# New instruction orders in a one-core conv-attention and recurrence kernel: the softmax and normalisation stages

## The reference

```python
x = x + conv(ln_c(x))                # x: 16 x 32 x 32 x 32, fp32
#   q, k, v = Wq x, Wk x, Wv x       (over channels c)
#   weight = softmax(q k / d + Gq q rq / d + Gk k rk / d)     over the last axis
#   conv   = weight (Gv1 v) + weight (Gv2 rv)
t = tokens(x)                        # 16 x 1024 tokens x 32
t = t + ffn(ln_t(t))                 # Wx = batchnorm(W ln_t(t)); y_t = sigmoid(Wx_t + V y_(t-1))
```

## Time and profile before

| | us |
|---|---|
| median of 3 runs | 154.19 (152.92 to 155.33) |
| time of the profiled execution | 154.99 |
| its span, first to last instruction | 153.1 |
| busy in the span: PE, DVE, ACT, POOL | 101.6, 96.2, 73.6, 61.9 |
| scores start (L990) | 40.13 |
| first addition of the softmax (L742) | 48.11 |
| first `weighted_sums` matmul (L1043) | 74.13 |
| first `residual` (L782) | 86.76 |
| last `bn_part` starts (L820) | 122.11 |

### The profile page before, as it was taken

How to read it: one execution, slowest core, us unless ns; L and a number is a source line. 1 busy time by engine, 2 the same in 40 slices (tenths; PEclk the granted TensorE clock), 3 DMA queues, 4 the chain that set the end, 5 groups by cost and what they waited for, 6 DMA issues and landing times.

```text
span 153.1 us, 4782 instructions
## 1 busy us (share of the span) xinstructions
PE 101.6 (66%) x2063; PEld 70.5 (46%) x2064; DVE 96.2 (63%) x158; ACT 73.6 (48%) x161; POOL 61.9 (40%) x62
## 2 busy tenths in 40 slices
PE   0769978686598880999755950358208987999400
PEld 0313312475588770888655950112002336999400
DVE  5996874000304879705501896379988969888992
ACT  8957786347700236692230030332343449999500
POOL 8995439840000687740500054555343000003940
PEclk9999999999779999599999999557965999999965
DMA  4880899899000002434332000000000000000467
GB/s 138 294 206 0 189 206 237 192 226 188 12 4 4 4 4 54 106 75 101 91 90 58 4 4 0 2 0 0 0 0 0 4 0 0 0 6 0 144 197 208
DMA packets 9825, 11.67 MB, mean 76 GB/s; under 512 B 2828, under 2 KB 6924, under 8 KB 9804
## 3 DMA queue, kind: packets, MB, share of 16 engines
q1 hardware_dynamic: 9612, 10.84, 28.0%
q10 hardware_dynamic: 192, 0.52, 1.4%
HBM read 2.97 MB, written 2.10 MB: 33 GB/s over the span
## 4 chain that ended last, share of the span: by engine, by line
DVE 27%; PE 18%; SPq 15%; ACT 13%; issue 11%; DMA 8%; POOL 5%; POOLq 0%; ACTq 0%
SPq L286 7%; PE ps L1033 5%; PE ps L990 5%; ACT warm L658 4%; DMA gates<-in_L_conv_Gk_dram 4%; SPq L291 4%; DVE xin L351 3%; DMA v_tile<-u_tile 3%; PE ps L1043 3%; DVE stat L786 3%; DVE y_tile L357 3%; DVE u_tile L782 2%; DVE rel_tile L816 2%; PE ps L1020 2%; ACT v_tile L658 2%
## 5 line engine op out<-in xcount | busy, mean ns | idle before, releaser
L1054 PE MATMUL ps<-rel_tile,w_bd 128*128 128x512 f32 x16 | 12.6, 888 | 10.9 <-DVE rel_tile L816 10.9
L357 POOL TENSOR_TENSOR y_tile<-xin,u_tile 128x256 f32<-128x256 f32 (+1 forms) x7 | 7.1, 1049 | 23.6 <-DVE xin L351 23.6
L990 PE MATMUL ps<-spread,v_tile 128*32 128x64 f32 x512 | 13.5, 269 | 4.4 <-DMA v_tile<-u_tile 3.0
L407 POOL TENSOR_TENSOR att_tile<-att_tile,soft 128x1024 f32<-128x1024 f32 x4 | 7.8, 1946 | 19.1 <-DVE soft L746 19.1
L990 PEld LDWEIGHTS ps<-spread,v_tile 128*32 128x32 f32 x512 | 12.6, 195 | 5.4 <-issue 4.5
L757 DVE TENSOR_TENSOR u_tile<-ps,xin 128x512 f32<-128x512 f32 x8 | 5.5, 684 | 15.0 <-PE ps L1033 15.0
L596 ACT ACTIVATE square<-y_tile 128x512 f32<-128x512 f32 x8 | 4.9, 629 | 18.4 <-POOL y_tile L428 18.4
L428 POOL TENSOR_TENSOR y_tile<-u_tile,stat 128x512 f32<-128x512 f32 x7 | 7.3, 1048 | 15.6 <-DVE stat L788 15.6
L1043 PE MATMUL ps<-spread,v_tile 128*32 128x64 f32 x512 | 9.2, 223 | 6.4 <-issue 6.4
L887 DVE TENSOR_SCALAR ps<-att_tile,bnv 128x512 f32<-128x512 f32 (+1 forms) x18 | 12.3, 762 | 1.2 <-ACT warm L658 1.1
L1020 PE MATMUL ps<-w_bd,y_tile 128*32 128x128 f32 x256 | 9.2, 307 | 5.0 <-ACT v_tile L510 5.0
(11 more groups left out here) (103 smaller groups left out, 234.1 us busy)
## 6 DMA issues: line engine op xcount, KB each, us to landing
spread<-rel_tile SPq DMA_DIRECT2D x32, 64.0 KB, 2.0
out_dram<-y_tile SPq DMA_DIRECT2D x8, 256.0 KB, 2.3
xin<-in_x_dram SPq DMA_DIRECT2D x3, 512.0 KB, 4.9
spread<-att_tile SPq DMA_DIRECT2D x12, 128.0 KB, 3.5
v_tile<-u_tile SPq DMA_DIRECT2D x12, 128.0 KB, 3.1
xin<-in_x_dram SPq DMA_DIRECT2D x2, 256.0 KB, 2.8
...
```

The costliest lines, as they stand in the source:

```text
L357: return eng.tensor_tensor(result[:, :, rows, :], back[:, at:at + P * k].rearrange("p (q i j) -> p q i j", q=Q, i=k), x2[:, :, rows, :], A ...
L407: nc.gpsimd.tensor_tensor(att_m[:, n, :, :], att_m[:, n, :, :], soft[:, 0, n, :].unsqueeze(2).broadcast_to([P, C, C]), ALU.subtract).then_ ...
L990: return nc.tensor.matmul(ps[group(g), first + j // 8, at:at + Q * HALF].rearrange("p (q i) -> p q i", q=Q), u_by_q[:, g, :, j], y_bd[:, : ...
L1054: nc.tensor.matmul(bank(WX_BANK[k % 2]), w_bd[:, 1, :], by_row(tokens, k), start=True, stop=True).then_inc(S["wx_product"], 1)
```

## The change

The order of calls is changed on every engine. The load of `rv` is issued after `regroup_u(2)`. The small multiplication that made a mean on DVE is gone: where DVE centres, one `scalar_tensor_tensor` computes sum * (-1/32) + x from the broadcast sum, and where POOL centres, POOL first makes the mean with a `tensor_scalar` on 128x32 or 128x16 and waits for it. `score_max` is split in two, `score_add` and `score_max`. The transfers of the weights are issued by SP, in both kernels and in the same order. The diff, cut to its core:

```diff
@@ block.sync
             spread_y(1)
-            for g in range(G):
-                sp.dma_start(rv_in[group(g), :], rv.rearrange("c h i -> c (h i)")).then_inc(S["rv_in"], 16)
             regroup_u(1)
             spread_y(2)
             spread_y(3)
             regroup_u(2)
+            for g in range(G):
+                sp.dma_start(rv_in[group(g), :], rv.rearrange("c h i -> c (h i)")).then_inc(S["rv_in"], 16)
@@ block.gpsimd
-            pool.wait_ge(S["ln_mean"], 3)
-            ln_centre(nc.gpsimd, 2, "ln_centred")
+            def ln_centre(n):
+                q = LN_PARTS[n][0]
+                pool.wait_ge(S["ln_sum"], n + 1)
+                nc.gpsimd.tensor_scalar(stat[:, 1, q, :], stat[:, 0, q, :], 1.0 / C, None, ALU.mult).then_inc(S["ln_mean"], 1)
+                pool.wait_ge(S["ln_mean"], q)
+                nc.gpsimd.tensor_tensor(centred[:, q, :, :], xin[:, q, :, :], stat[:, 1, q, :].unsqueeze(2).broadcast_to([P, C, C]),
+                                        ALU.subtract).then_inc(S["ln_centred"], 1)
...
             def centre(k):
+                pool.wait_ge(S["t_sum"], k + 1)
+                nc.gpsimd.tensor_scalar(stat2[:, 1, k, :], stat2[:, 0, k, :], 1.0 / C, None, ALU.mult).then_inc(S["t_mean"], 1)
                 pool.wait_ge(S["t_mean"], k + 1)
...
             centre(1)
+            centre(2)
+            centre(3)
             scale(0)
-            centre(2)
             scale(1)
-            centre(3)
             scale(2)
@@ block.scalar
             t_std(3)
+            t_square(4)
+            t_square(5)
+            t_std(4)
             wx_out(0)
+            t_std(5)
             wx_out(1)
...
@@ block.vector
-                dve.wait_ge(S["ln_sum"], n + 1)
-                dve.wait_ge(S["nought_set"], 1)
-                nc.vector.scalar_tensor_tensor(out=stat[:, 1, q, rows], in0=stat[:, 0, q, rows], scalar=1.0 / C,
-                                               in1=nought[:, 0:k], op0=ALU.mult, op1=ALU.add).then_inc(S["ln_mean"], 1)
...
+                nc.vector.scalar_tensor_tensor(out=centred[:, q, rows, :],
+                                               in0=stat[:, 0, q, rows].unsqueeze(2).broadcast_to([P, k, C]), scalar=-1.0 / C,
+                                               in1=xin[:, q, rows, :], op0=ALU.mult, op1=ALU.add).then_inc(S["ln_centred_dve"], 1)
...
+            score_add(0)
             score_max(0)
+            score_add(1)
             score_max(1)
             weight_sum(0)
+            score_add(2)
             weight_sum(1)
             score_max(2)
+            score_add(3)
             score_max(3)
             weight_sum(2)
-            relv_out(0)
-            relv_out(1)
             weight_sum(3)
...
-                dve.wait_ge(S["t_sum"], k + 1)
-                nc.vector.scalar_tensor_tensor(out=stat2[:, 1, k, :], in0=stat2[:, 0, k, :], scalar=1.0 / C,
-                                               in1=nought[:, 0:HALF], op0=ALU.mult, op1=ALU.add).then_inc(S["t_mean"], 1)
                 if k == UNITS - 1:
-                    nc.vector.tensor_tensor(unit(x2n, k), unit(x2, k),
-                                            stat2[:, 1, k, :].unsqueeze(2).broadcast_to([P, HALF, C]),
-                                            ALU.subtract).then_inc(S["t_centred_dve"], 1)
+                    nc.vector.scalar_tensor_tensor(out=unit(x2n, k), in0=stat2[:, 0, k, :].unsqueeze(2).broadcast_to([P, HALF, C]),
+                                                   scalar=-1.0 / C, in1=unit(x2, k), op0=ALU.mult, op1=ALU.add
+                                                   ).then_inc(S["t_centred_dve"], 1)
@@ block.tensor
-            for n in range(4):
+            for n in range(PIECES4):
                 relative_values(n)
             pe.wait_ge(S["score_sum"], CHUNKS)
             pe.wait_ge(S["att_in0"], 16 * Q * G)
             weighted_sums(0, range(C)).then_inc(S["wsum_product"], 1)
-            for n in range(4, PIECES4):
-                relative_values(n)
```

More of the change, by code:

```diff
@@ L170, in side_bank @@
             return bank(SIDE[n % 2])
-        def ln_centre(eng, n, done):
-            q, row, k = LN_PARTS[n]
-            eng.tensor_tensor(centred[:, q, row:row + k, :], xin[:, q, row:row + k, :],
-                              stat[:, 1, q, row:row + k].unsqueeze(2).broadcast_to([P, k, C]),
-                              ALU.subtract).then_inc(S[done], 1)
         def ln_scale(eng, n, done):
@@ L572, in _ @@
             score_exp(1)
-            turn_weights(0)
-            turn_weights(1)
             value_out(0)
             value_out(1)
-            score_exp(2)
+            turn_weights(0)
             value_out(2)
             value_out(3)
+            turn_weights(1)
+            value_out(4)
+            score_exp(2)
+            value_out(5)
+            value_out(6)
             score_exp(3)
-            value_out(4)
-            value_out(5)
+            value_out(7)
             turn_weights(2)
-            value_out(6)
-            value_out(7)
             turn_weights(3)
@@ L682, in ln_mean, with ln_centre @@
                 nc.vector.tensor_reduce(stat[:, 0, q, rows], xin[:, q, rows, :], AX_X, ALU.add).then_inc(S["ln_sum"], 1)
+            def ln_centre(n):
+                q, row, k = LN_PARTS[n]
+                rows = slice(row, row + k)
                 dve.wait_ge(S["ln_sum"], n + 1)
-                dve.wait_ge(S["nought_set"], 1)
-                nc.vector.scalar_tensor_tensor(out=stat[:, 1, q, rows], in0=stat[:, 0, q, rows], scalar=1.0 / C,
-                                               in1=nought[:, 0:k], op0=ALU.mult, op1=ALU.add).then_inc(S["ln_mean"], 1)
+                nc.vector.scalar_tensor_tensor(out=centred[:, q, rows, :],
+                                               in0=stat[:, 0, q, rows].unsqueeze(2).broadcast_to([P, k, C]), scalar=-1.0 / C,
+                                               in1=xin[:, q, rows, :], op0=ALU.mult, op1=ALU.add).then_inc(S["ln_centred_dve"], 1)
             def ln_sum2(n):
@@ L702, in ln_out @@
                 ln_scale(nc.vector, n, "y_ready_dve")
-            ln_mean(0)
-            dve.wait_ge(S["ln_mean"], 1)
-            ln_centre(nc.vector, 0, "ln_centred_dve")
-            ln_mean(1)
-            dve.wait_ge(S["ln_mean"], 2)
-            ln_centre(nc.vector, 1, "ln_centred_dve")
-            ln_mean(2)
+            ln_sum(0)
+            ln_centre(0)
+            ln_sum(1)
+            ln_centre(1)
+            ln_sum(2)
             ln_sum2(0)
@@ L716, in _ @@
             ln_out(1)
-            ln_mean(3)
+            ln_sum(3)
             ln_sum2(2)
@@ L824, in _ @@
             residual(2)
+            residual(3)
             t_sum2(0)
-            residual(3)
+            t_sum2(1)
             t_rstd(0)
-            t_sum2(1)
+            t_sum2(2)
             t_rstd(1)
-            t_sum2(2)
+            t_sum2(3)
+            t_rstd(2)
+            t_rstd(3)
+            residual(4)
+            residual(5)
             t_turn(0)
-            t_rstd(2)
-            t_sum2(3)
-            t_rstd(3)
             t_turn(1)
-            residual(4)
+            t_sum2(4)
             t_turn(2)
-            residual(5)
+            t_rstd(4)
+            t_sum2(5)
             t_turn(3)
+            t_rstd(5)
+            residual(6)
+            residual(7)
             bn_part(0)
-            residual(6)
-            t_sum2(4)
+            t_sum2(6)
             bn_part(1)
-            t_rstd(4)
-            residual(7)
-            t_sum2(5)
-            t_rstd(5)
-            bn_part(2)
-            t_turn(4)
-            t_sum2(6)
             t_rstd(6)
             t_sum2(7)
+            t_turn(4)
+            t_rstd(7)
+            bn_part(2)
             t_turn(5)
             bn_part(3)
-            t_rstd(7)
             t_turn(6)
```

31 lines of the change are left out of this document (11 added, 20 removed).

## The result

The change makes the kernel faster: 145.75 us (median of 4 runs, 145.43 to 146.24) against 154.76 (4 runs, 152.92 to 155.95), a ratio of 0.949 with the interval 0.941 to 0.958. The medians here are of all runs, while each ratio and its interval leave out the runs that lie more than 1.5% above the fastest of their kernel, so the two don't divide exactly. The median is 9.0 lower where 11.5 was forecast; the range holds it. The profiled execution has a span of 144.4 against 153.1. In the table "moved by" counts from the start of the span; what each stage itself gained or lost stands behind it.

What follows compares the result with a forecast made beforehand. Bounds were taken stage by stage: SP's issue queue and full DMA engines, engine order and PE supply gaps, then a busy DVE. -2.0 - 5.1 - 4.4 = -11.5 from 154.99 gives 143.5, median 142.7; range 139.5 to 147.0.

Steps and rivals of the forecast that it cites:

- Term 1: Regrouping: with `rv` behind `regroup_u(2)`, SP issues each later group sooner and scores start earlier; -2.0 us, ends 0 and -2.6.
- no gain, no loss: First normalisation: five means leave DVE, but SP's queue still starts with ACT's work behind the gates, so time is unchanged.
- Term 2: From the scores to `residual(0)`: new orders bring `residual(0)` at 81.7 instead of 86.76; -5.1 us, ends +0.3 and -8.2.
- walk: The prediction's step-by-step timing of softmax, values and second normalisation, on the clock of the trace before.
- Term 3: Second normalisation, to the end of the fifth turn: 23.8 instead of 28.24; -4.4 us, ends -1.2 and -6.9.
- The hold that I added: Second normalisation: one DVE instruction held up by POOL's centring, as in the trace before; 0.5 us added.
- Behind the fifth turn: PE's four projections and last statistics, 7.8 us before the change, were to stay as they are: no difference.
- rival 5: Recurrence at the low clock: PE's clock stays 0.5 when round 1 starts; slower, 159.0 us, chance 0.03.
- Rival 1: Regrouping: ACT's transfers or the last spread of y set the landing, Term 1 is 0; 144.7 us, chance 0.10.
- Rival 2: Second normalisation keeps its waits, POOL becomes the bound and Term 3 gives 1.2; 145.9 us, chance 0.15.
- Rival 3: PE stands before the relative pieces because `weigh(3)` stays late, Term 2 is +0.3; 148.1 us, chance 0.07.
- Rival 4: Weighted sums in one run stream without supply gaps, Term 2 gains 3.1 more; 139.6 us, chance 0.03.

Runs made afterwards that it cites:

- e2_rv_back: Changed kernel with the load of `rv` moved back ahead of `regroup_u(1)`; 145.15 us.
- e4_act_back: Changed kernel with ACT's old order in the softmax, the first two turns ahead of the first value copy; 149.67 us.
- e3_pe_back: Changed kernel with PE's old order, relative pieces 4 to 7 between the two weighted sums; 147.83 us.
- e8_att_act: Changed kernel with ACT instead of SP issuing the last eight of 32 weight transfers; 145.92 us against 145.52.
- e10_both: Changed kernel with ACT issuing the last eight weight transfers and 12 instead of 4 fillers behind the last residual; 143.65 us.
- e9_fill: Changed kernel with 12 instead of 4 filler matmuls behind the last residual; 143.65 us against 145.52.
- e12_warm: Changed kernel with 12 late fillers, one more ahead of `project_u(0)`, the two before `project_u(1)` left out; 142.20 us, ratio 0.920 to the kernel before.

## Why the prediction was right, and where not

*Term 1 (-2.0; measured -1.35 in the profile, about 0 in the time).* The step that failed is "SP is late for each later group". Without `rv` SP comes to `regroup_u(1)` at 21.53, and u is there at 22.70: PE's fillers and its later start became the bound. The sentence that in the first normalisation there is "no gain, no loss" failed with it. The new POOL mean and the later arrival of x moved POOL's centring, which holds DVE's scaling. By the rule of the Trainium skill (SBUF — State Buffer, section "Who interferes with whom") named in the prediction, the trace agrees at this place, 0.85 of hold (1.54 for 0.69), which I had looked for only at `centre(7)`; there it didn't occur (0.69, no hold). And an earlier start of the scores need not reach the end: e2_rv_back has them at 40.82 and `residual(4)` no later than the changed kernel.

*Term 2 (-5.1; measured -5.1 from the scores on).* Right in size and in its steps up to `residual(0)`: turned by 69.1 (walk with the -1.35: 69.0), first weighted sum at 72.41 (72.5), `residual(0)` at 80.27 (80.3). e4_act_back and e3_pe_back show that ACT's and PE's orders each carry most of it, 6.3 to 6.9 and 4.3 to 4.8 when taken away alone, so they don't add. The queue of SP was mis-sized. "SP issues 32 in 24.02 including 5 of waiting" misreads the waits: of the 5.2 that SP waited for ACT's turns, 3.7 lay before the first issue at 58.24, and only 1.5 within the 24.02. A last landing at 82.4, with the 2.0 from issue to landing of the page before, left 22.2 for the 32; in the profile now they wait for nothing and still take 25.80, six of them 1.2 to 1.6 each where before there were three such, and they begin 0.75 later. So the last transfer came about 4 later than in the walk.

*Term 3 (-4.4; measured -3.3).* The work was 21.35 in the walk and 21.54 in the trace; the waits 2.45 and 3.4. Nearly all of the miss is the queue of term 2: the walk had `weighted_sums(1)` end near 90, before DVE wants `residual(4)`; in truth DVE stands 2.3 there. With the transfers in time (e8_att_act, e10_both) the stretch takes 23.3 and 23.2, where the walk without the hold had 23.3. The hold that I added never came.

*Behind the fifth turn (0; measured +1.1).* "The four are as close after the change: no difference" was the second failure. Before, the clock was at 0.5 when the fifth projection started and came back during the four. Now the fifth projection still ran at 1.00 (two records in 1.12), after a pause of 3.28, and then the clock fell, so that the last three ran at 0.50 throughout, 5.49 for six records. e9_fill and e12_warm show it: with fillers in the pause, 3.17 and a stretch of 6.7. This is rival 5's mechanism, seen in one stretch and not in the recurrence, whose 30.2 did not change.

*The rivals.* Rival 1 is out as a mechanism: in both profiles the chain into the scores ends with SP's last issue of u and its landing (5.14 behind it before, 5.40 now), although its price, nothing for term 1, is close to what the time shows. Rival 2 is out, since term 3 gave 3.3 and POOL waits for DVE (1.80 before its fifth mean at 93.39). Rival 3 is out: `weigh(3)` ends at 67.9, not 75.5. Rival 4 (no supply gaps) is out: the gaps are 1.29 and 1.88 in one run of weighted sums, and the eight pieces in a row did not change the pace. That the gaps are instruction supply was only argued; if they are, the rule of the Trainium skill that such crossings are mostly hidden (Runtime: NRT & Kernel Launch, "Instruction fetch mechanics") is not what this kernel shows.

The sum: -1.35 - 5.1 - 3.3 + 1.1 = -8.7 where -11.5 was said; 0.65 of the difference is term 1, 1.1 term 3 (the transfers, in the main), 1.1 the clock. There is some luck in the range: 145.75 lies above the forecast's own 139.5 to 144.5, and the wider range holds it because it took in rivals 1 and 2, of which neither happened as a mechanism.
